# Two-layer gated attention and expert network on one core: another way to route tokens in layer 1's attention steps

## What is computed

```python
E = where(mask, -inf, Q @ K.T); A = softmax(E / 8); x = x + (A @ V @ W_O) * gate
h = layernorm(x)
probs = softmax(h @ gate_w.T)                      # 32 experts
topk_w, topk_idx = top_k(probs, 4)
topk_w = topk_w / sum(topk_w)
# each token is written into the buffers of its 4 experts: at row "how many came before
# it at that expert", up to 256 rows an expert; later ones are dropped
slot = minimum(pos, 256)
buf = zeros(32, 257, 256).at[expert, slot].set(h[token])
# then: silu(gate) * up, down, times topk_w, added to the token's row; a shared expert beside it
```

## Time and profile before

| | |
|---|---|
| median of 3 runs | 1052.3 us (1049.78, 1052.3, 1059.98) |
| profiled execution, its span | 1055.6 us |
| PE busy | 895.3 us (85%) |
| DVE busy | 648.2 us (61%) |
| POOL busy | 551.9 us (52%) |
| ACT busy | 495.7 us (47%) |
| chain that ended last, largest parts | DVE 18%, POOL 8%, PE 7%, issue 7%, DMA 6%, ACT 2% |
| its largest lines | DVE att L2038 4%, DVE attT_lo L2026 2%, DVE mx L2011 2% |

### The profile page before, as it was taken

One profiled execution on the slowest core, in us unless ns is written; L12 is line 12 of the kernel. 1 busy time (PEld: TensorE's weight loads), 2 busy tenths in 40 slices (PEclk: granted clock), 3 DMA queues, 4 the chain that ended last, 5 costly groups with the idle time before them and its releaser, 6 DMA issues. The chain is left out here.

```text
span 1055.6 us, 18563 instructions
## 1 busy us (share of the span) xinstructions
PE 895.3 (85%) x5465; PEld 753.2 (71%) x5465; DVE 648.2 (61%) x2128; ACT 495.7 (47%) x1781; POOL 551.9 (52%) x634
## 2 busy tenths in 40 slices
PE   4998768999998598888459899999999978999940
PEld 3563447888887488787358799999999966888720
DVE  4603034787787555464258889999999963444441
ACT  1313663444442244454257667877887741222200
POOL 1400122576677135455546866666666653877861
PEclk8978988999999798899779999999999979999985
DMA  9621875589889667986298944514426204899688
GB/s 307 201 94 51 247 209 142 129 250 253 267 237 272 209 209 220 252 300 216 96 227 206 247 122 170 177 65 152 117 66 197 85 14 115 156 222 246 80 201 162
DMA packets 157812, 189.70 MB, mean 180 GB/s; under 512 B 16035, under 2 KB 137017, under 8 KB 157714
## 3 DMA queue, kind: packets, MB, share of 16 engines
q1 hardware_dynamic: 109810, 121.87, 39.9%
q0 software_dynamic: 30720, 46.46, 20.5%
q10 hardware_dynamic: 17184, 20.19, 5.7%
HBM read 96.19 MB, written 103.63 MB: 189 GB/s over the span
## 5 line engine op out<-in xcount | busy, mean ns | idle before, releaser
L1875 POOL DMA_INDIRECT slots_d<-rows,place x128 | 133.4, 1042 | 65.7 <-DVE place L2095 34.5
L1934 ACT ACTIVATE att<-bank,mx 128x77 f32<-128x77 f32 x512 | 160.9, 360 | 1.2 <-DVE mx L2011 1.1
L997 POOL DMA_INDIRECT y_d<-rows x78 | 77.6, 995 | 96.3 <-DVE rows L1375 71.5
L1934 ACT ACTIVATION_READ_ACCUMULATOR att<-bank,mx 128x1 f32 x512 | 123.6, 241 | 0.0
L957 POOL DMA_INDIRECT slots_d<-rows,place x64 | 63.9, 998 | 19.0 <-issue 18.8
L1397 PE MATMUL bank<-wd_hi,act_hi 128*128 128x256 f32 (+1 forms) x206 | 68.5, 332 | 2.7 <-DVE act_lo L1370 1.4
L1889 POOL DMA_INDIRECT acc_d<-expert_out,target_rows x32 | 49.6, 1551 | 26.2 <-issue 25.4
L1399 PE MATMUL bank<-wd_hi,act_lo 128*128 128x256 f32 (+1 forms) x206 | 60.1, 292 | 0.0
L1398 PE MATMUL bank<-wd_lo,act_hi 128*128 128x256 f32 (+1 forms) x206 | 60.0, 291 | 0.0
L2011 DVE TENSOR_REDUCE mx<-bank 128x6 f32<-128x462 f32 (+1 forms) x96 | 55.3, 576 | 5.6 <-PE bank L2195 5.2
L1889 POOL DMA_INDIRECT result<-expert_out,target_rows x32 | 49.5, 1547 | 16.9 <-DMA result<-expert_out,target_rows 8.1
(11 more groups left out here) (322 smaller groups left out, 2998.2 us busy)
## 6 DMA issues: line engine op xcount, KB each, us to landing
rows<-slots_d SPq DMA_DIRECT2D x39, 260.0 KB
slots_d<-zrow SPq DMA_DIRECT2D x8, 1168.0 KB
expert_rows<-slots_d SPq DMA_DIRECT2D x32, 292.0 KB
expert_gate_up<-in_wgu SPq DMA_DIRECT2D x28, 256.0 KB
x_res<-y_d POOLq DMA_DIRECT2D x14, 512.0 KB
wqk_d<-wqk SPq DMA_DIRECT2D x32, 154.0 KB
vwo_d<-vwo SPq DMA_DIRECT2D x16, 308.0 KB
x_res<-in_x SPq DMA_DIRECT2D x8, 512.0 KB
```

The lines of the kernel that those rows point to most:

```text
L997: pool.indirect_dma_start(y0_d, bass.IndirectOffsetOnAxis(ap=x_rows(s)[:, b, D:D + 1].bitcast(I32), axis=0), y_rows(s, b), None, bounds_ch ...
L1875: pool.indirect_dma_start(slots_d, bass.IndirectOffsetOnAxis(ap=place[:, n % 3, k:k + 1], axis=0), rows[:, n % 3, :], None, bounds_check=S ...
L1934: last = act.activation(att[:, par, h * S:(h + 1) * S], bank[:, a, i * S:(i + 1) * S], ACT.Exp, scale=-1.0, bias=mx[:, par, h:h + 1], accu ...
```

## The change

Six things, all in the steps of layer 1's attention:

1. The logits are no longer copied from PSUM to `lg1`. `max`, `match_replace` and the exponential read them where the router left them, `logits1`.
2. The negative maximum `ngm` is made by ScalarE instead of VectorE, and the router's exponential goes behind the last four exponentials of the step, where it also waits for `msel_ready`. TensorE's positions, which write to the same bank, now wait for `ew_ready` too.
3. `mselb` and `cum` are both made from `tk` by one instruction each, without a wait between them.
4. The chosen experts are marked by the matrix: `tri` has ones up to and at the diagonal's row, and 16384 (`CHOSEN`) on the diagonal, so that a chosen expert's position is larger by 16384. The multiplication with `mselb` is gone; `max` of all 32 takes the chosen ones. The buffers begin at row `SLOT0` = 16640 of `slots_d`, which grows from 8448 to 24832 rows of 1168 bytes; what is cleared, written and read of it stays as much as before.
5. `max` writes the integers itself, into `place` with eight columns, and comes ahead of the largest of the first six heads; the cast is gone. `cum` begins at 2 (e + 1) instead of zero, which the product with `allone` turns into 256 (e + 1), so that the third product is gone.
6. The weights come at the step's end, behind the scaling of the last 4 heads, and the last of their instructions is a `scalar_tensor_tensor`.

Ahead of the first step GpSimd makes one more `affine_select` for `tri`, `cum` by `iota` instead of `memset`, and `ones1` by `memset` instead of `ebase` by `iota`.

The core of the diff:

```diff
-                        pool.memset(cum[:, 0, :], 0.0).then_inc(c3, 1)
+                        pool.iota(cum[:, 0, :], pattern=[[CAP // P, E1]], base=CAP // P, channel_multiplier=0,
+                                  allow_small_or_imprecise_dtypes=True).then_inc(c3, 1)
...
+                        pool.wait_ge(c3_zero, 2)
+                        pool.affine_select(out=tri[:], in_=tri[:], compare_op=ALU.not_equal, fill=float(CHOSEN), base=0,
                                            pattern=[[1, P]], channel_multiplier=-1).then_inc(c3, 1)
...
                         if routes:
-                            act.wait_ge(ngm_ready, n - 1)
-                            act.activation(ew[:, par, :], lg1[:, par, :], ACT.Exp, bias=ngm[:, par, :]).then_inc(ew_ready, 1)
+                            act.wait_ge(top_ready, n - 1)
+                            act.activation(ngm[:, par, :], t8[:, par, 0:1], ACT.Copy, scale=-1.0).then_inc(ngm_ready, 1)
                         if scores:
                             exps(n, par, 2)
+                        if routes:
+                            act.wait_ge(ngm_ready, n - 1)
+                            act.wait_ge(msel_ready, n - 1)
+                            act.activation(ew[:, par, :], logits1, ACT.Exp, bias=ngm[:, par, :]).then_inc(ew_ready, 1)
...
                             dve.wait_ge(pos_read, m + 1)
-                            picked = chain.mark(dve.tensor_tensor(slot[:, mp, :], slot[:, mp, :], mselb[:, mp, :], ALU.mult))
+                            want(dve, sent[m % 3], 16 * K1 * (m // 3))
+                            dve.max(place[:, m % 3, :], slot[:, mp, :]).then_inc(place_ready, 1)
                         if scores:
                             largest(n, par, 0)
-                        if dispatch:
-                            chain.need(picked)
-                            picked = chain.mark(dve.max(slot8[:, mp, :], slot[:, mp, :]))
                         if routes:
                             norm_b(r, par)
-                        if dispatch:
-                            chain.need(picked)
-                            want(dve, sent[m % 3], 16 * K1 * (m // 3))
-                            dve.tensor_copy(place[:, m % 3, :], slot8[:, mp, 0:K1]).then_inc(place_ready, 1)
...
                             dve.wait_ge(r_mm, r + 1)
-                            dve.tensor_copy(lg1[:, par, :], bank[:, 7, 256:256 + E1]).then_inc(r_out, 1)
...
-                            dve.tensor_scalar(ngm[:, par, :], t8[:, par, 0:1], -1.0, None, ALU.mult).then_inc(ngm_ready, 1)
+                            dve.max(t8[:, par, :], logits1).then_inc(top_ready, 1)
...
-                            took = chain.mark(dve.tensor_scalar(mselb[:, par, :], tk[:, par, :], NEG, None, ALU.is_equal))
-                            chain.need(took)
-                            dve.tensor_tensor(cum[:, 1 - par, :], cum[:, par, :], mselb[:, par, :], ALU.add)\
-                               .then_inc(msel_ready, 1)
+                            dve.scalar_tensor_tensor(mselb[:, par, :], tk[:, par, :], NEG, ones1[:], ALU.is_equal, ALU.mult)
+                            dve.scalar_tensor_tensor(cum[:, 1 - par, :], tk[:, par, :], NEG, cum[:, par, :],
+                                                     ALU.is_equal, ALU.add).then_inc(msel_ready, 1)
...
                             pe.wait_ge(msel_ready, m + 1)
+                            pe.wait_ge(ew_ready, m + 1)
                             to = bank[:, 7, 288:288 + E1]
                             pe.matmul(to, tri[:], mselb[:, mp, :], start=True, stop=False)
-                            pe.matmul(to, allone[:], cum[:, mp, :], start=False, stop=False)
-                            pe.matmul(to, onerow[0:1, :], ebase[0:1, :], start=False, stop=True).then_inc(pos_mm, 1)
+                            pe.matmul(to, allone[:], cum[:, mp, :], start=False, stop=True).then_inc(pos_mm, 1)
```

51 lines of the change are left out of this document (25 added, 26 removed).

## The result

The changed kernel took 1059.1 us (median of 12 runs) beside 1051.1 us for the kernel before on the same chip (12 runs): ratio 1.0066, 95% interval 1.0042 to 1.0090. On another chip it was 1.0096 (1.0069 to 1.0123). So it is slower by 0.7 to 1%, some 7 to 10 us, where I had forecast 2.3 us faster; it is outside of my range.

The account below looks back on a forecast made before the run. It took each 9.66 us step as bound by VectorE and a TensorE-ScalarE loop equally long; the longest new loop, 9.56, saves 0.10 in 23 steps, 2.3 us, giving 1050.0 us from 1052.3, range 1044 to 1057.

Parts of the forecast that it names:

- VectorE as the limit, 9.66 us a step: Layer 1's attention steps before the change: the chain of waits names VectorE's scaling once a step, 23 periods of 9.66 us.
- the other reading of the prediction: Same steps before the change: a loop between TensorE and ScalarE through `xbT` is as long, 9.71 us by its pieces.
- What the parts cost by themselves: VectorE's own sum in a step: at most 0.59 us removed, 9.66 to 9.07; reading PSUM costed at nothing.
- The loops at 9.50, 9.55 and 9.62: Three engine loops of the changed step; the longest sets its length, taken as 9.56 us.
- loop 1: TensorE and ScalarE through `xbT`: 9.61 less the removed third position product's slot of 0.11, so 9.50 us.
- loop 2: TensorE and ScalarE through `ew`, new: positions wait for the router's exponential, now last on ScalarE; 9.55 us.
- Loop 3: ScalarE and VectorE through the weights, new, now behind the last four exponentials; 9.62 us, or 9.51 with the new last instruction.
- The row that I called the one on which the forecast rests: A late step with VectorE relieved: TensorE's first product with the values goes from 838.41 to 848.02, still 9.61 us.
- my 0.10: Forecast gain per step, 9.66 to 9.56 us; over 23 steps 2.3 us, with bounds 0.9 to 3.7.
- The indirect DMAs start over a microsecond earlier; nothing of the steps waits for them … Together I take these as zero: Effects around the steps, including GpSimd's earlier indirect DMAs, whose buffer is wanted only three steps later; cost taken as zero.
- The slower rival, through `ew`: TensorE's positions wait for a late `ew`; 0.37 us later makes steps 9.92 and the kernel 1058 us; chance 0.14.
- The rival of the larger `slots_d`: Outside the steps: `slots_d` three times as large moves other buffers in DRAM, either sign, some 1%; chance 0.08.

Follow-up runs that it names:

- e14: The kernel before with only the first of the four indirect DMAs of a step; ratio 0.9884 to the kernel before, period 9.61 us.
- e6: The changed kernel with only the first of the four indirect DMAs of a step; ratio 0.9828 to the kernel before, period 9.42 us.
- e4: The changed kernel with the integer places made late again, behind the normed row; ratio 0.9958 to the kernel before, again 0.9982, period 9.61 us.
- e2: The kernel before with only the early places added, made by `max` ahead of the first reduction; ratio 1.0107 to the kernel before, period 10.34 us.
- e3: The changed kernel with the router's exponential `ew` back ahead of the last four exponentials; ratio 1.0062 to the kernel before, period 10.32 us.
- e10: The changed kernel with places made late and `ew` back between the exponentials; ratio 0.9966 to the kernel before, period 9.70 us.
- e8: The changed kernel with all four indirect DMAs held until VectorE has the step's last maxima; ratio 1.0128 to the kernel before, period 10.43 us.
- e11: The changed kernel with two of the four indirect DMAs of a step; ratio 0.9974 to the kernel before, period 9.94 us.

## Why the prediction was wrong

**VectorE as the limit, 9.66 us a step: right, but not alone.** The chain of waits of the kernel before runs through VectorE and GpSimd's root for layer B from 630 to 830 us. Those 9.66 are not a sum of VectorE's instructions alone: it is busy for 37.88 us in 40, that is 9.15 a step, and waits 0.2 a step for `rstd_b`. e14 shows that the other reading of the prediction, a TensorE and ScalarE loop of nearly the same length, was right as well: 9.60.

**What the parts cost by themselves: right.** `MAX8` on PSUM takes 0.20, as on SBUF. With one indirect DMA, where nothing else disturbs, VectorE is busy for 37.75 us in 40 in the old code and 36.45 in the new; times the periods, 37.75 / 40 x 9.61 = 9.07 and 36.45 / 40 x 9.42 = 8.58, so 0.49 us a step are gone, where I had written at most 0.59.

**The loops at 9.50, 9.55 and 9.62: mis-sized.** e6 has the whole change with all three loops in it, and takes 9.41. In loops 1 and 2 the removed product was under-priced. I took its own slot, 0.11. From the start of the first position product to that of the second product of the scores it is 0.58 us in the kernel before and 0.36 in e6, so its removal is worth 0.22: loop 1 is 9.61 - 0.22 = 9.39 and loop 2 9.44, still a little over. Loop 3 is the one on which e6's chain of waits lies, except that it crosses from ScalarE to VectorE behind the twelfth exponential, at the scaling of 12 heads, and not behind the sixteenth; it measures 9.41, not 9.51 to 9.62. The row that I called the one on which the forecast rests, 9.61 us, had the right length, since e14 has 9.60; but in that step the chain of waits of the kernel before runs through ScalarE and VectorE and not through TensorE, so it did not measure the loop that I took it for.

With the releases of the transposes and the router on time, the change is worth 9.68 to 9.61 in e4 (0.07 a step) and, with one indirect DMA, 9.60 to 9.41 (0.19); my 0.10 lies between, partly by luck, since it comes from loops that were too long.

**"The indirect DMAs start over a microsecond earlier; nothing of the steps waits for them … Together I take these as zero": this is the step that failed.** The first half is right: they start 1.1 us earlier against the transposes, and nothing waits for their data. But what they do to others while they are made is not in the view of who waits for whom. Moved by 1.1 us, the second lies over the release of the transposes and the third over that of the router. Where I had put zero, it costs 0.5 to 0.7 us a step (period 10.15 and 10.34 against 9.68) and turns 2.3 us less into 7 to 10 us more. e2 is the direct proof: that one move in the kernel before costs 1.1%, although it saves VectorE a cast as well.

**The slower rival, through `ew`: the sign and the wait, but not the cause.** I wrote that a wait at the positions with a period above 9.66 would mean that it holds. The period is there, and the wait in about half of the steps, 6.2 us in 9 waits; and yet e3, which takes that loop away, is as slow. `ew` is late because ScalarE is, and ScalarE is because the transposes' release is. A wait that a forecast names may still only pass on a delay from elsewhere; one has to follow it back.

**The range, the last rival and the rule.** The range, 1044 to 1057, had no case in which a start moved without a waiter cost anything. The rival of the larger `slots_d` falls with e4, which has it and is no slower than the kernel before; e2 is slow without it. The early steps, which I expected unchanged within 1 us, took 75.1 us before and 73.5 and 75.0 after in their first seven periods. The rule of the Trainium skill ("VectorE: DVE Perf Modes", section "Rules for kernel authors") that chained operations are to be counted as instructions fits VectorE's own saving, 0.49 us for four instructions fewer; that the step falls with it no run shows: the most that came was 0.19 of 0.49 us, since another limit stands at 9.41.

## What to carry to other kernels

When a change moves the start of work on a queue that nobody waits for, ask not only who waits for it but what runs beside it now, and look there in the new trace. If an engine's next instructions start on time and yet its reader waits, the release is late, not the work; the chain of waits then shows the engine with too long a time for its form (1.97 us for 0.63 us of matmuls). To find which part of a change costs, apply each part alone to the kernel before and take each alone out of the changed one: four kernels here made a square in which one factor explained everything.

## What the runs showed of the hardware

TensorE's releases came late by 0.2 to 1.6 us, and now and then by about 2, when they fell due between the start of an indirect DMA of 128 rows that GpSimd made directly behind another one and about 2.1 us later. Its own matmuls kept their pace of 0.12 us. The Trainium skill ("SBUF — State Buffer", section "Who interferes with whom") states, of the engines' ports to SBUF, that TensorE and ScalarE never wait on anyone; for the starts of TensorE's matmuls this trace agrees, but of when their results are released the sentence says nothing, and that is where the time went.

- A single indirect DMA, while made and while its rows were on their way, delayed none of 250 releases in e6.
- Late releases came at fixed times, counted from the start of the indirect DMA in whose time they fell, and not by a fixed delay. In the changed kernel the transposes', due 0.4 to 0.8 us behind the start of the second one, came at 1.3 to 1.4 or at 2.1; the router's, due 0.1 to 0.6 behind the third, all but one at 1.5 to 1.6. The product with the values came 1.9 to 2.2 us behind the start of the fourth, whether it was due at 1.5 (before, e4, e10) or at 0.4 (e8). It looks as if a release were held up to a point of GpSimd's work: the earlier it falls due within that time, the later it is.
- Not every release was held. Those due up to 1.6 us behind the first indirect DMA of a row, when the second has just been started, were nearly all on time, the others 0.15 us late at most. The router, due 0.3 to 0.8 us behind the second one, was on time in the kernel before and in e4, while the transposes, due 0.6 to 0.9 behind it, were late by 0.7 in e11, and those of the exponentials, due at 0.5, in most steps of the changed kernel. What else takes part was not found.
- The length of the rows did not matter (32 or 1168 bytes); the number of indirect DMAs in a row did. That and the fixed times point at the making of them on GpSimd and not at their data. What it shares with TensorE's release no run shows: whether the last writes to PSUM or the count itself was held up can't be told from this trace.
- Four in a row started 1.4, 1.3 and 1.3 us apart in nearly every kernel.
